# Layer 1 of a two-layer conditioned attention block: K's exponentials with bias and sums on ScalarE, K-V products by 64-column tiles, new x's norm at the front of the step

## What is computed

```python
xn = _ln(x, ln_w, ln_b)
q = xn @ Wq + bq
k = xn @ Wk + bk + (1.0 - src_mask) * -1000000.0
q = softmax(q.reshape(b, t, h, dh), axis=-1)
k = softmax(k.reshape(b, t, h, dh), axis=1)       # over the 128 rows of a sequence
v = ((xn @ Wv + bv) * src_mask).reshape(b, t, h, dh)
att = einsum('bnhd,bnhl->bhdl', k, v)             # one 64 x 64 matrix a head
y = einsum('bnhd,bhdl->bnhl', q, att).reshape(b, t, d)
scale, shift = split((silu(emb) @ W_emb + b_emb)[:, None, :], 2, axis=2)
hh = _ln(y, ln2_w, ln2_b) * (1.0 + scale) + shift
return x + silu(hh) @ W_out + b_out
```

## Time and profile before

| | |
|---|---|
| median of 3 runs | 1174.09 us (1173.89 to 1174.12) |
| the profiled execution | 1175.47 us, its span 1173.5 us |
| TensorE busy (products) | 1091.3 us, 93% |
| VectorE busy | 807.6 us, 69% |
| ScalarE busy | 556.8 us, 47% |
| GpSimd busy | 469.7 us, 40% |

### The profile page before, as it was taken

How to read it: one execution, slowest core, us unless ns; L and a number is a source line. 1 busy time by engine, 2 the same in 40 slices (tenths; PEclk the granted TensorE clock), 3 DMA queues, 4 the chain that set the end, 5 groups by cost and what they waited for, 6 DMA issues and landing times.

```text
span 1173.5 us, 25383 instructions
## 1 busy us (share of the span) xinstructions
PE 1091.3 (93%) x8426; PEld 929.7 (79%) x8426; DVE 807.6 (69%) x1393; ACT 556.8 (47%) x1726; POOL 469.7 (40%) x783
## 2 busy tenths in 40 slices
PE   5989999999999999999767999999999999999995
PEld 2788888888888888888654788888888888888884
DVE  4357766666776666776546587788777777787774
ACT  3267666787666678766661222223323332223221
POOL 3123344434333443433322245544444445455532
PEclk9989999999999999999979899999999999999998
DMA  7301111011111101120244301111111111101111
GB/s 249 144 22 60 49 50 56 22 58 58 58 46 50 56 22 58 58 60 25 81 135 149 109 9 46 55 54 54 54 54 54 54 54 53 35 34 38 54 37 54
DMA packets 44767, 72.40 MB, mean 62 GB/s; under 512 B 8624, under 2 KB 12816, under 8 KB 44720
## 3 DMA queue, kind: packets, MB, share of 16 engines
q1 hardware_dynamic: 44720, 71.80, 18.8%
HBM read 54.97 MB, written 16.79 MB: 61 GB/s over the span
## 4 chain that ended last, share of the span: by engine, by line
PE 66%; DVE 11%; POOL 9%; issue 7%; ACT 4%; POOLq 1%; DVEq 0%; DMA 0%; ACTq 0%; SPq 0%
PE bank L1268 16%; PE bank L1269 15%; PE bank L1270 15%; PE bank L1321 4%; DVE stat L919 3%; PE bank L1311 3%; PE bank L1334 3%; POOL stat L502 3%; DVE y_s L972 2%; POOL z_s L537 2%; PE bank L1263 1%; ACT room L678 1%; PE bank L1392 1%; DVE s_lo L994 1%; POOL stat L500 1%
## 5 line engine op out<-in xcount | busy, mean ns | idle before, releaser
L1268 PE MATMUL bank<-xt_hi,w_hi 128*128 128x256 f32 x768 | 226.1, 294 | 0.4 <-DVEq L880 0.4
L1269 PE MATMUL bank<-xt_lo,w_hi 128*128 128x256 f32 x768 | 216.5, 282 | 0.0
L1270 PE MATMUL bank<-xt_hi,w_lo 128*128 128x256 f32 x768 | 215.9, 281 | 0.0
L670 ACT ACTIVATE prob<-prob,neg_max 128x128 f32<-128x128 f32 x512 | 198.5, 395 | 12.9 <-DVE neg_max L947 12.8
L499 POOL TENSOR_SCALAR stat<-stat 128x1 f32<-128x1 f32 x128 | 34.5, 269 | 370.1 <-DVE stat L923 357.7
L689 ACT ACTIVATE th<-z_s 128x512 f32<-128x512 f32 x64 | 40.3, 630 | 272.8 <-POOL z_s L537 272.8
L1268 PE MATMUL bank<-w_hi,xt_hi 128*128 128x512 f32 x384 | 158.4, 413 | 0.0
L542 POOL TENSOR_TENSOR x_res<-x_res,bias_wide 128x512 f32<-128x512 f32 x64 | 90.5, 1414 | 161.2 <-DMA x_res<-between_layers 150.0
L1270 PE MATMUL bank<-w_hi,xt_lo 128*128 128x512 f32 x384 | 151.6, 395 | 0.0
L1269 PE MATMUL bank<-w_lo,xt_hi 128*128 128x512 f32 x384 | 151.6, 395 | 0.0
L1268 PEld LDWEIGHTS bank<-xt_hi,w_hi 128*128 128x128 f32 x768 | 147.0, 191 | 3.6 <-issue 1.1
(11 more groups left out here) (117 smaller groups left out, 2274.3 us busy)
## 6 DMA issues: line engine op xcount, KB each, us to landing
x_in<-in_x_dram SPq DMA_DIRECT2D x32, 256.0 KB, 2.7
x_res<-in_x_dram SPq DMA_DIRECT2D x32, 256.0 KB, 2.8
between_layers<-x_res SPq DMA_DIRECT2D x32, 256.0 KB, 2.0
x_in<-between_layers SPq DMA_DIRECT2D x32, 256.0 KB, 2.8
x_res<-between_layers SPq DMA_DIRECT2D x32, 256.0 KB, 3.0
out_dram<-x_res SPq DMA_DIRECT2D x32, 256.0 KB, 2.9
prob<-in_L_cond_emb_w_dram SPq DMA_DIRECT2D x8, 512.0 KB, 7.5
prob<-in_L_cond_W_emb_dram SPq DMA_DIRECT2D x8, 512.0 KB, 6.6
```

The costliest lines, as they stand in the source:

```text
L670: last = act.activation(prob[:, b, i, :], prob[:, b, i, :], ACT.Exp, bias=neg_max[:, b, i:i + 1], accum_out=row_sum[:, b, h:h + 1])
L1268: pe.matmul(o, hi, w_h, start=first, stop=False)
L1269: pe.matmul(o, hi, w_l, start=False, stop=False)
L1270: return pe.matmul(o, lo, w_h, start=False, stop=stop)
```

## The change

K's bias is written straight into `k_exp`, and `k_tmp` is gone. VectorE takes the negated maximum only. ScalarE takes the exponential in 4 pieces of 128 with that maximum as bias, and each piece's sum as its accumulator, so subtract and sums leave VectorE. `keys_values` makes 8 products of 64 by 64 columns instead of 4 of 128 by 128, each pair on the two column halves of the array. In GpSimd's and VectorE's lists the norm of x of group n moves to the front of the step.

```diff
--- before.py
+++ after.py
@@ GpSimd, step, layer 1
                     else:
+                        if n:
+                            norm1(n, 0)
                         if k:
                             residual(k, 0)
                             norm2(k, 0)
+                        if n:
+                            norm1(n, 1)
                         if f:
                             v_mask(f, slot, 0)
                         if k:
                             norm2(k, 1)
                             add_shift(k, 0)
-                        if n:
-                            norm1(n, 0)
-                            norm1(n, 1)
-                        if k:
                             add_shift(k, 1)
@@ ScalarE
                 def k_bias(f, slot, pair):
...
-                    act.wait_ge(*done(s[f"ksub{pair}"], f + (-GROUP)))
-                    kt = k_tmp[:, pair, :].rearrange("p (c n) -> p c n", c=2)
+                    act.wait_ge(*done(s["kt_pe"], f + (-GROUP - 1)))
+                    kt = k_exp[:, slot, pair * D:(pair + 1) * D].rearrange("p (c n) -> p c n", c=2)
...
                 def k_exps(f, slot, pair):
-                    act.wait_ge(*done(s[f"ksub{pair}"], f))
-                    v = k_exp[:, slot, pair * D:(pair + 1) * D]
-                    act.activation(v, v, ACT.Exp).then_inc(s[f"kexp{pair}"].sem, GROUP)
+                    act.wait_ge(*done(s[f"kmax{pair}"], f))
+                    act.wait_ge(*done(s["krec"], f + (-2 * GROUP)))
+                    v = k_exp[:, slot, pair * D:(pair + 1) * D].rearrange("p (g n) -> p g n", n=P)
+                    for i in range(2 * GROUP):
+                        last = act.activation(v[:, i, :], v[:, i, :], ACT.Exp, bias=k_max[:, pair, i:i + 1],
+                                              accum_out=k_sum[:, slot, pair, i:i + 1])
+                    last.then_inc(s[f"kexp{pair}"].sem, GROUP)
@@ VectorE
                 def k_soft(f, slot, pair):
                     dve.wait_ge(*done(s[f"kbias{pair}"], f))
-                    kt = k_tmp[:, pair, :].rearrange("p (g n) -> p g n", n=P)
-                    km = k_max[:, pair, :]
-                    dve.tensor_reduce(km, kt, AX.X, ALU.max).then_inc(s[f"kmax{pair}"].sem, GROUP)
-                    dve.wait_ge(*done(s[f"kmax{pair}"], f))
-                    dve.wait_ge(*done(s["kt_pe"], f + (-GROUP - 1)))
-                    dve.wait_ge(*done(s[f"ksum{pair}"], f + (-2 * GROUP)))
-                    dve.tensor_tensor(k_exp[:, slot, pair * D:(pair + 1) * D].rearrange("p (g n) -> p g n", n=P), kt,
-                                      km.rearrange("p (g o) -> p g o", o=1).broadcast_to([P, 2 * GROUP, P]),
-                                      ALU.subtract).then_inc(s[f"ksub{pair}"].sem, GROUP)
-
-                def k_sums(f, slot):
+                    dve.wait_ge(*done(s[f"kexp{pair}"], f + (-GROUP)))
+                    dve.tensor_reduce(k_max[:, pair, :], k_exp[:, slot, pair * D:(pair + 1) * D].rearrange("p (g n) -> p g n", n=P),
+                                      AX.X, ALU.max, negate=True).then_inc(s[f"kmax{pair}"].sem, GROUP)
+
+                def k_inverse(f, slot):
                     for pair in range(2):
                         dve.wait_ge(*done(s[f"kexp{pair}"], f))
-                        dve.tensor_reduce(k_sum[:, slot, pair, :],
-                                          k_exp[:, slot, pair * D:(pair + 1) * D].rearrange("p (g n) -> p g n", n=P),
-                                          AX.X, ALU.add).then_inc(s[f"ksum{pair}"].sem, GROUP)
-                    for pair in range(2):
-                        dve.wait_ge(*done(s[f"ksum{pair}"], f))
                     dve.wait_ge(*done(s["att_out"], f + (-GROUP - 1)))
                     dve.reciprocal(k_rec[:, slot].rearrange("p a g -> p (a g)"),
...
                 def step1(n, f, k, late, slot):
                     if late:
                         output(late, 1)
+                    if n:
+                        stats1(n, 0)
                     if k:
                         kv_out(k, 1 - slot, 0)
...
                     if f:
                         k_soft(f, slot, 1)
+                    if n:
+                        stats1(n, 1)
+                    if f:
                         v_add(f, slot, 0)
                     if k:
                         y_norm(k, 1 - slot, 1)
-                    if n:
-                        stats1(n, 0)
-                        stats1(n, 1)
...
@@ TensorE, keys_values
                     for c in range(C):
-                        last = pe.matmul(bank[bk["KV"][b]][:, c * P:(c + 1) * P], k_tok[b][:, c * P:(c + 1) * P],
-                                         v_s[:, kslot, b, c * P:(c + 1) * P], start=True, stop=True)
+                        for h in range(2):
+                            rows = slice(DH1 * h, DH1 * (h + 1))
+                            head = slice(c * P + DH1 * h, c * P + DH1 * (h + 1))
+                            last = pe.matmul(bank[bk["KV"][b]][rows, head], k_tok[b][:, head], v_s[:, kslot, b, head],
+                                             start=True, stop=True, tile_position=(0, DH1 * h))
```

More of the change, by code:

```diff
@@ L191, in build @@
         q_exp = room[:, 0, :].rearrange("p (s b d) -> p s b d", s=2, b=GROUP)
-        k_tmp = room[:, 2, 0:2 * D].rearrange("p (s d) -> p s d", s=2)
         q_tmp = room[:, 2, 2 * D:3 * D]
@@ L236, in build @@
                  "pv_out")
-        only1 = ("kt_pe qt_pe kt_out qt_out att_pe att_out kbias0 kbias1 kmax0 kmax1 ksub0 ksub1 kexp0 kexp1 ksum0 ksum1 krec "
+        only1 = ("kt_pe qt_pe kt_out qt_out att_pe att_out kbias0 kbias1 kmax0 kmax1 kexp0 kexp1 krec "
                  "q_pe q_add qmax qsub qexp qsum qrec")
@@ L1123, in step1 @@
                         y_norm(k, 1 - slot, 1)
-                    if n:
-                        stats1(n, 0)
-                        stats1(n, 1)
-                        if not f:
-                            low_parts(1, (2,))
+                    if n and not f:
+                        low_parts(1, (2,))
                     if k:
@@ L1141, in step1 @@
                     if f:
-                        k_sums(f, slot)
+                        k_inverse(f, slot)
                     if k:
```

## The result

| | before | changed |
|---|---|---|
| median, us | 1173.99 (1171.51 to 1174.12, 4 runs) | 1143.82 (1142.86 to 1145.71, 4 runs) |
| profiled execution, us | 1175.47 | 1145.71 |
| its span, us | 1173.5 | 1143.9 |
| step of layer 1, us | 31.86 | 29.76 |

The ratio is 0.9747, with a 95% interval of 0.9732 to 0.9762. The sign and the place were right; one term of the sum, the K-V product by tiles, had the wrong sign.

The account below looks back on a forecast made before the run. Layer 1's chain through norms and shifts was taken to set the step; chain and TensorE's list both came to 30.4 us against 31.86. Fourteen steps save 20.4, less 0.8 outside: 19.5 us, 1154.6 us median, range 1146 to 1168.

Parts of the forecast that it names:

- the K-V product by tiles: TensorE's 64-column products: weight loads bound them, so no gain, and change-over adds 0.2 us a sequence, 0.4 a step.
- What bounds the kernel: Layer 1: TensorE's list with short holes, 1.87 us a step; without them 30.0 of 31.86 us.
- The chain: Path from `query(k,0)` through norms and GpSimd's two shifts to the next K projection sets the step: 31.98 us, then 30.4.
- The exponentials on ScalarE, at nothing: Four pieces of 128 on ScalarE take 1.6 to 2.4 us a set, costed at nothing because later work covers them.
- The norm at the front: GpSimd's `norm1(n,0)` fits in idle time; VectorE's `stats1(n,0)` waits for the load but ends before `query(k,0)` needs `kv_out`.
- the 1.5 us that I had to spare: VectorE's `kv_out(k,0)` ends near 900.0 us, while `query(k,0)` needs it at 901.5.
- VectorE's relief: Two subtractions and two sums of K's softmax leave VectorE, 3.5 us of a step.
- The change-over: TensorE entering and leaving the tile form: 0.11 us for leaving, about as much for entering, 0.2 a sequence.
- A: Rival: column halves overlap, K-V product 0.6 us, TensorE's list 29.4, chain 29.9, 1146 us; chance 0.2.
- B: Rival: GpSimd's `norm1(n,1)` is late, hole before `output(k,0)` or second `turn_yn`, step 31.0 to 31.6, 1163 to 1171; chance 0.2.
- C: Rival: loads and products one after the other, 1.6 us a K-V product, about no gain, 1174 us; chance 0.04.
- D: Rival: VectorE waits for x's load at the front, delaying `query(k,0)`; 1191 us if it lands at 7 us; chance 0.04.

Follow-up runs that it names:

- no_tiles: The changed kernel with the K-V product put back to 4 products of 128 by 128 columns; 1147.79 us, a step of 29.95 us.
- mask_late: The changed kernel with GpSimd's `v_mask(f,0)` moved from ahead of `norm2(k,1)` to behind the first shift; 1140.94 us, a step of 29.63 us.
- tiles_norm: The changed kernel with K's softmax (subtraction and sums) back on VectorE, tiles and moved norms kept; 1167.46 us, a step of 31.31 us.
- only_norm: The kernel before the change with only the norms of x moved to the front; 1170.30 us, a step of 31.56 us.

## Why the prediction was right in its place and wrong in its size

**What bounds the kernel.** Right. The time went out of the holes of layer 1's steps and of nothing else: 14 x 2.10 = 29.4 of 29.7 us. TensorE's list without holes was put at 30.0, by adding 0.17 us of overlap to each drawn hole; `no_tiles`, whose remainder ahead of `output(late,1)` is 0.05 us in the mean, has 29.95.

**The chain.** Right in its order and nearly in every size. The norm took its undisturbed 1.99 us (2.04 forecast). The first shift stands 17.92 us behind the K projection's start (18.4 forecast), the second 22.54 (23.05), and from there to the next K projection it is 908.82 - 901.49 = 7.33, as forecast. Of the 0.51 us that the chain is early by, 0.38 is what `query(k,0)` is early by (7.25 behind the K projection's start, 7.63 forecast), and that is the K-V product ahead of it; 0.13 lies in the rest. One link of the recorded sum does not add up, and was right all the same: 907.0 and 2.04 and 1.0 give 910.04 for `norm2(k,1)`, not 910.2. Those two pieces took 894.85 - 891.69 = 3.16 us, near the 3.2 that the sum has.

**The exponentials on ScalarE, at nothing.** Right, and at the lower bound: 0.39 us of pitch. **The norm at the front.** Right: VectorE waits for the load there, about 1 us as a rule and twice 2.0, and none of it comes through. The changed kernel's waits between 640 and 1143 us (sum, count, longest):

```profile
DVE stat L922 <- DMA x_in<-between_layers: 13.9, 13, 2.0
```

Eleven of the 13 are 0.77 to 1.09 us. The two others, 1.95 at 734.24 and 2.01 at 1062.71, are longer than the 1.5 us that I had to spare, yet `kv_out(k,0)` ends 1.0 and 0.8 us ahead of `query(k,0)` there too. **VectorE's relief** was 2.9 us a group and not 3.5, ScalarE's load 2.05, inside 2 to 3.5.

**The step that failed: "So I take the loads as the bound: no gain, and the change-over into and out of the tile form comes on top ... 0.2 us a sequence, 0.4 a step."** Measured is -0.18 and -0.11 us, -0.29 a step in TensorE's list and -0.19 in the step. A forecast step of 30.4 against 29.76 is 0.64 x 14 = 9.0 us. In TensorE's list the term alone is 0.40 + 0.29 = 0.69 too long (the whole list was forecast at 30.4, and is 29.67 in `mask_late`), and in the chain, which in fact sets the step, it is 0.38 of the 0.64. The rest of the 0.64 is the 0.13 of the chain and a flaw of measure: the 30.4 was a step from K projection to K projection, to be set against 31.98, and I took it off the 31.86 of the reciprocals, 0.12 x 14 = 1.7 us. Outside the full steps 4 products cost +0.8 in the forecast; by the measured 0.18 and 0.11 I estimate -0.6, 1.4 us more. That is 10.4 us, and the forecast missed by 10.8. With the term as measured and all else as recorded, the list is 29.7 and the chain 30.0: 14 x 1.86 + 0.6 = 26.6 us less, 1147.5, inside my range, and 3.7 us from the measured time.

The reason given, "Both that and today's K-V product load 8 x 128 = 1024 weight columns", compared the amounts of two rows that were both consistent with one serial stream of loads. I said that the earlier trace rows allows both readings, and took the one that made the gain nothing. The merged row does allow both, but the trace it comes from does not. This is the row in a window that ends at 318.27, and in one that ends at 318.30:

```profile
318.14 0.32 PE L1334 MATMUL bank<-room,v_s 128*32 128x128 f32 x4
318.14 0.43 PE L1334 MATMUL bank<-room,v_s 128*32 128x128 f32 x8
```

Four instructions start within 0.020 us, none for the next 0.11, then four more, and from there on four every 0.109 us: the four column tiles run at once in the kernel before already. The change-over itself is real, 0.09 us on entering (0.53 against 0.44 behind the four turns), and is inside the numbers above.

**The rivals.** A happened: its block of 0.6 us is the measured 0.62, its step 29.9 the measured 29.76, its 1146 missed by 2 us. Part of that is luck: it took 0.6 us off TensorE's list, where 0.29 came off, and it is the chain that brought the step to 29.9. It had a chance of 0.2, where the starts in the trace spoke for it. B did not happen in the changed kernel; `tiles_norm` and `only_norm` show its hole, 0.86 and 0.87 us ahead of the second `turn_yn`, where the subtraction still stood ahead of the norm. C is refuted even for the worst order (0.90 us a product, not 1.6). D's wait exists and is covered.

## What to carry to other kernels

Where a merged row of the trace is explained equally well by "the loads bound it" and by "the tiles overlap", it bears out neither: look at the row in narrow windows, to see when its single instructions start. Where that does not decide either, put the difference into the range and give both about the same chance. When products are cut into column tiles, order them so that neighbours use different column halves: the order alone was worth 0.28 us of 0.90 in one block. And cost two edits on one chain together: the norm's move and the subtraction's removal were worth 4.2 and 7.2 us alone and 27.5 with both.

## What the runs showed that I had not expected

- Float32 products on 64-column tiles: each column half takes an instruction every 0.058 us, with 64 moving columns and with 32, and the two halves run at once. The order sets only how far apart they start, 0.006 us or 0.287. The full 128-column form takes 0.89 us for 8 instructions, 0.112 each, for the same weights.
- More tiles do not by themselves cost more: 16 instructions in 0.62 us against 8 in 0.89. In the bad order they cost as much as the 8 (0.90).
- Fusing subtraction, exponential and sum by bias and accumulator costs ScalarE 0.39 us per 128 columns, its accumulator's read of 0.19 hidden; for that a 1.1 us subtraction and a 0.64 us sum left VectorE for each set.
- GpSimd needs 1.6 us a group less for the same instructions: over the span 7.7 us less with the exponentials moved alone, 11.4 with the norms moved alone, 25.3 in the changed kernel. Its norm took 1.99 us there; before, the pair between the shifts took 5.36, the first of them 3.36 and the second 2.00. That VectorE's operations beside it make the difference is likely by this, and not shown.
